# A one-core Perceiver kernel: TensorE multiplies the identity by itself in 24 of its waits

## The reference

```
x = x + _L0_xattn_ref(ctx_1024, _layernorm(x), ...)         # cross attention to 1601 context rows, 16 heads of 64
x = x + _L0_attn_ref(_layernorm(x), ...)                    # selective scan, inner width 256, state 16
x = x + _L0_ffn_ref(_layernorm(x), ...)                     # 4-head attention, then 8 experts, top 2, one shared
x = x + _L1_xattn_ref(ctx_1024, _layernorm(x), mask, ...)   # cross attention, masked
x = x + _L1_attn_ref(_layernorm(x), ...)                    # convolution, state space model, 4 heads, state 64
x = x + _L1_ffn_ref(_layernorm(x), ...)                     # gated feed-forward, inputs and weights rounded to FP4
return x
```

## Time and profile before

| | us |
|---|---|
| median of 3 runs | 2292.67 |
| lowest, highest | 2290.51, 2299.47 |
| profiled execution | 2296.36 |
| its span | 2294.70 |
| TensorE busy in it | 2030.7 (88%) |
| VectorE, ScalarE, GpSimd busy | 1696.9, 1365.7, 566.2 |
| mean granted clock of TensorE | 0.943 of full |

### The profile page before, as it was taken

One profiled execution on the slowest core, in us unless ns is written; L12 is line 12 of the kernel. 1 busy time (PEld: TensorE's weight loads), 2 busy tenths in 40 slices (PEclk: granted clock), 3 DMA queues, 4 the chain that ended last, 5 costly groups with the idle time before them and its releaser, 6 DMA issues. The chain is left out here.

```text
span 2294.7 us, 36359 instructions
## 1 busy us (share of the span) xinstructions
PE 2030.7 (88%) x10794; PEld 1094.3 (48%) x10794; DVE 1696.9 (74%) x4252; ACT 1365.7 (60%) x2461; POOL 566.2 (25%) x584
## 2 busy tenths in 40 slices
PE   5798989998999999979777899999999999997845
PEld 4254535353545354533355354544545454544543
DVE  5778787878787878479656777777786868775456
ACT  3366666666666667644322587778686867776202
POOL 3424343333333331039300201121111111120000
PEclk9799999999999999979888899999999999999877
DMA  2111111111111110023102011111111111100000
GB/s 76 46 46 45 46 46 45 45 45 45 45 45 45 45 45 31 31 70 135 57 1 102 6 35 50 34 53 34 34 34 34 34 34 34 34 31 17 1 10 9
DMA packets 40896, 95.07 MB, mean 41 GB/s; under 512 B 11436, under 2 KB 26776, under 8 KB 40760
## 3 DMA queue, kind: packets, MB, share of 16 engines
q1 hardware_dynamic: 40760, 93.61, 12.0%
HBM read 65.15 MB, written 27.92 MB: 41 GB/s over the span
## 5 line engine op out<-in xcount | busy, mean ns | idle before, releaser
L1063 DVE TENSOR_TENSOR x_p_lo<-x_psum,x_p_hi 128x512 f16<-128x512 f32 (+2 forms) x896 | 605.7, 682 | 207.0 <-ACT x_psum L854 192.4
L853 ACT ACTIVATE x_p_hi<-x_psum 128x512 f16<-128x512 f32 (+2 forms) x480 | 287.9, 600 | 266.2 <-PE x_psum L696 264.4
L716 PE MATMUL x_psum<-x_p_hi,x_x_both 128*128 128x512 f16 (+1 forms) x832 | 318.8, 383 | 58.9 <-DVE x_p_lo L1063 58.7
L853 ACT ACTIVATE x_p_hi<-x_psum,x_bcol 128x512 f16<-128x512 f32 (+1 forms) x416 | 292.3, 703 | 103.9 <-PE x_psum L696 101.6
L694 PE MATMUL x_psum<-x_q,x_xT_both 128*128 128x512 f16 x832 | 320.2, 385 | 6.5 <-DMA x_q<-x_shift_rows 6.5
L695 PE MATMUL x_psum<-x_q,x_xT_both 128*128 128x512 f16 x832 | 318.8, 383 | 0.0
L696 PE MATMUL x_psum<-x_q,x_xT_both 128*128 128x512 f16 x832 | 318.6, 383 | 0.0
L717 PE MATMUL x_psum<-x_p_lo,x_x_both 128*128 128x512 f16 (+1 forms) x832 | 317.8, 382 | 0.0
L718 PE MATMUL x_psum<-x_p_hi,x_x_both 128*128 128x512 f16 (+1 forms) x832 | 317.6, 382 | 0.0
L854 ACT ACTIVATE x_psum<-x_psum 128x512 f32<-128x512 f32 (+2 forms) x480 | 287.3, 598 | 0.6
L1006 DVE CUSTOM_DVE_ANT_0 x_junk<-x_psum,x_brow 128x512 bf16<-128x512 f32 (+2 forms) x512 | 280.1, 586 | 4.7 <-PE x_psum L769 3.8
(11 more groups left out here) (431 smaller groups left out, 3103.3 us busy)
## 6 DMA issues: line engine op xcount, KB each, us to landing
context_rows<-x_x_both SPq DMA_DIRECT2D x16, 832.0 KB, 3.5
context_cols<-x_xT_both SPq DMA_DIRECT2D x16, 832.0 KB, 5.9
x_xT_both<-context_cols SPq DMA_DIRECT2D x16, 832.0 KB, 4.5
x_x_both<-context_rows SPq DMA_DIRECT2D x16, 832.0 KB, 6.3
x_raw<-in_ctx SPq DMA_DIRECT2D x16, 768.0 KB
ssm_c_row<-ssm_bc_rows SPq DMA_DIRECT2D x16, 512.0 KB, 4.2
ssm_b_wide<-ssm_bc_rows SPq DMA_DIRECT2D x7, 512.0 KB, 3.6
x_mrow<-in_mask_BxS_bk SPq DMA_DIRECT2D x16, 200.1 KB
```

The source lines that it names most:

```text
L716: pe.matmul(out, v_hi, p_hi[r][rows, :], start=start, stop=False)
L853: act.activation(p_hi[r][rows, :], score[r][rows, :], ACT.Exp, scale=SCORE_UNIT, **bias).then_inc(p_hi_ready, 1)
L1063: v.tensor_tensor(p_lo[r][rows, :], score[r][rows, :], p_hi[r][rows, :], ALU.subtract).then_inc(p_lo_ready, 1)
```

## The change

A new function issues n float32 products of `ident` with itself, 128 columns each, to one place in a PSUM bank, each overwriting the last. Nobody reads the results, no semaphore is counted, and the next real product into the bank overwrites it. It is called at 20 places of TensorE's code. Two of these are in `cross_attention` with other counts for the masked block, so that 24 calls run, with 371 products. No other engine's code is changed.

```diff
+def keep_clock(pe, bank, ident, n):
+    for _ in range(n):
+        pe.matmul(bank[:, 0:P], ident[:, :], ident[:, :], start=True, stop=True)
...
@@ cross_attention @@
+                    keep_clock(pe, slot_psum[3], ident, 24 if masked else 10)
                     pe.wait_ge(fold_ready, 1)
...
                     pe.wait_ge(lat_ready, 1)
                     pe.wait_ge(prep_dve, 8)
+                    keep_clock(pe, slot_psum[3], ident, 0 if masked else 8)
                     pe.wait_ge(prep_act, 9)
...
                         ins = pe.transpose(slot_psum[1][:, t * P:(t + 1) * P], latx[:, t, :], ident[:, :])
                     ins.then_inc(prep_ready, 1)
+                    keep_clock(pe, slot_psum[3], ident, 8)
...
@@ attention_loop @@
                 if kind == "turn":
+                    if isinstance(at, Pre):
+                        keep_clock(pe, aux[:, 512:1024], ident, 14)
                     pe.wait_ge(m_ready, at.n + 1)
...
                     aux_item(at, item)
+                keep_clock(pe, acc[0], ident, 14)
                 for u in range(AHEAD):
                     scores(u, 0, 0, 0, 0)
...
@@ selective_scan @@
+                keep_clock(pe, slot[1], ident, 12)
                 pe.wait_ge(in_in, 16)
...
                 ins.then_inc(in_turned, 1)
+                keep_clock(pe, slot[1], ident, 6)
                 pe.wait_ge(rest_in, 48)
...
                 ins.then_inc(turned, 1)
+                keep_clock(pe, slot[1], ident, 5)
                 pe.wait_ge(fold_ready, 1)
...
@@ expert_block @@
+                keep_clock(pe, slot[3], ident, 22)
                 pe.wait_ge(heads_in, HEADS_IN)
...
                 ins.then_inc(turned, 1)
+                keep_clock(pe, slot[3], ident, 5)
                 pe.wait_ge(wt_ready, 1)
...
                 product(slot[3], WT[:, K4, :], nxT, k_made)
+                keep_clock(pe, slot[0], ident, 5)
...
+                keep_clock(pe, slot[1], ident, 28)
                 pe.wait_ge(xf_ready, 1)
...
                 ins.then_inc(xf_turned, 1)
+                keep_clock(pe, slot[1], ident, 5)
                 pe.wait_ge(xfT_ready, 1)
...
@@ state_space_block @@
+                keep_clock(pe, slot[3], ident, 24)
                 pe.wait_ge(matrices_in, MATRICES_IN)
...
+                keep_clock(pe, slot[3], ident, 5)
                 pe.wait_ge(wt_ready, 3)
...
+                keep_clock(pe, slot[2], ident, 36)
                 pe.wait_ge(yn_ready, 1)
...
                     ins.then_inc(y_turned, 1)
+                keep_clock(pe, slot[1], ident, 10)
                 pe.wait_ge(yg_ready, 2)
...
@@ fp4_block @@
+                keep_clock(pe, slot[3], ident, 60)
                 pe.wait_ge(u_ready, 1)
...
                 ins.then_inc(u_turned, 1)
+                keep_clock(pe, slot[3], ident, 30)
                 pe.wait_ge(wq_ready, 1)
...
                 ins.then_inc(w_turned, 1)
+                keep_clock(pe, slot[3], ident, 4)
                 pe.wait_ge(w_out, 2)
```

## The result

| | before | changed |
|---|---|---|
| median of 6 runs each, us | 2294.89 | 2278.07 |
| lowest, highest | 2290.51, 2303.24 | 2275.24, 2283.43 |
| profiled execution (span) | 2296.36 (2294.70) | 2277.59 (2275.9) |
| mean granted clock | 0.943 | 0.969 |
| TensorE busy | 2030.7 | 2092.7 |

The changed kernel takes 0.9926 of the time, 95% interval 0.9911 to 0.9941: 17 us less (14 to 20), under one per cent. The sum of the prediction was 14.9 and its forecast 2278. The three runs of the kernel before on which the forecast was built have a median of 2292.67; the six here have 2294.89.

The account below looks back on a forecast made before the run. Most stage-end stretches were taken as engine-to-engine chains with TensorE at half clock. Terms 3.4 + 4.0 + 3.7 + 3.0 + 1.4 + 1.7 - 1.0 - 1.3 = 14.9 us, from median 2292.67 to 2278; range 2269 to 2289.

Parts of the forecast that it names:

- late and early places: Late: expert block's later part, state-space end, last block, 11.1 us gained; early: block starts and maxima's turns, 3.8 us.
- Late part 3.7: Expert block, 28 products ahead of 1166.10: transposes 1.97 to 0.97, product 6.26 to 3.60, 3.7 us gained.
- Start 3.0: Expert block's start, 22 products: 3.9 us gained if the clock holds, nothing if it falls; taken as 3.0.
- End 4.0, start 0: State-space block: end gains 4.0 us (1.3 transposes, 2.7 matmuls); start gains 0, between -2 and +1.5.
- The sum said 3.4: Last block: transposes gain 1.1 us and the first two steps of lines 2156 and 2157 gain 2.3, together 3.4.
- After that the vector engine sets the pace: Last block, after the quantization at 2256.45: the vector engine sets the pace; total gain stays 3.4 us.
- a term of 1.4: Scan's start, 12 products: matmuls of 994.11 shorten from 6.92 to 5.3 us; gain taken as 1.4, between -1.5 and +2.5.
- turn and scores -1.3: Second attention block: products ahead of the maxima's turn cost 1.9 us, first exponential comes 0.6 earlier, net loss 1.3.
- +1.0 said: First attention block: 0.3 - 0.8 + 1.4 - 1.9, the last for the maxima's turn, a loss of 1.0 us.
- 0.3 - 0.8 + 1.4 = 0.9: First attention block's start: first 10 products gain 0.3 us, 8 ahead of 39.04 cost 0.8, the next 8 gain 1.4.
- that same load hides it: First attention block, 14 products behind the turn: scores run at full clock, but the raw-context load hides that gain.
- The falling clock: Rival: clock falls in the 1 to 2 us between products and work; 7 of 15 us stay, 2286; chance 0.19.

Follow-up runs that it names:

- e_early: Changed kernel without the products of the late places, so only those at the five block starts and two turns; 2292.27 us, 0.9976 of the kernel before.
- e_late_shift: Kernel before with the late places' products and, of the early ones, only the 14 behind the turn of the maxima; 2291.04 us, 0.9971 of the kernel before.
- e_late: Kernel before with only the late places' products (28, 5, 36, 10, 60, 30, 4); 2284.94 us, 0.9949 of the kernel before.
- e_plus: Changed kernel with counts removed or trimmed at starts and turns, and products added ahead of attention outputs and the last four tiles; 2277.04 us, 0.9915 of the kernel before.
- e_overrun: Changed kernel with 16 more products in each of three late waits (44, 52, 46 for 28, 36, 30); 2285.79 us, 0.9958 of the kernel before.
- the repeat: Changed kernel run once more, unaltered; 2275.96 us, 0.9919 of the kernel before.
- e_long_only: Changed kernel without the short runs of 4 to 10 products in scan, expert, state-space and last blocks; 2288.05 us, 0.9966 of the kernel before.
- e_transpose: Changed kernel with each added product replaced by two float32 transposes of the identity; 2278.91 us, 0.9917 of the kernel before.

## Why the prediction was right, and where it was not

**The forecast and its mechanism** held: a gain of 14.9 against 17 (14 to 20), and the split into late and early places, 11.1 and 3.8, against 11.7 and 5.5. That 2278 meets 2278.07 to a tenth of a microsecond is luck: the three runs it was counted from lie 2.2 us below the median of the six, and misses of several us in single blocks cancel. The late places' 11.7 is in part luck too, since 2.7 us of its profile's gain lie in a block without products.

**Expert block.** Late part 3.7: the block differs by 3.8 between e_early and the changed kernel. Start 3.0: the scores' matmuls come 14.19 us after entry for 18.67, 4.5 earlier, but 0.9 of it is the weights' landing, 6.03 for 6.93, which is no doing of the products. Some 0.8 is given back until `xf` is turned: TensorE pauses 1.47 us with nothing to wait for, and the 16 transposes behind run at half, 3.51 for 1.97. Against e_late_shift, with the same landing, the start is worth 2.8. (The prediction's good case was added up as 3.9; its terms, 1.7 and 2.4, make 4.1.)

**State-space block.** End 4.0, start 0, measured 3.9 together, 4.4 in e_late with the end alone and 0.8 the other way in e_early with the start alone. The 24 products end 2.5 us past the former landing (2111.89 is 8.08 after entry, 5.52 before), and line 1871 begins 0.4 later, as bounded.

**Last block.** The sum said 3.4, and at the fifth tile it was that (37.83 us after entry for 41.17). The step that failed is "After that the vector engine sets the pace": the end is TensorE's again, and the clock, kept in the profile before over an idle 3.32, fell behind 3.48 in the changed kernel. 1.4 of the 3.4 were lost; e_plus got them back. Since e_early lost the same 1.4 without any product in this block, and e_overrun lost the clock over the very same 3.32, these 1.4 us are not shown to come from the change: it may be the one profile of the kernel before that was lucky.

**Scan.** 12 matmuls 5.51 for 6.92, their end 1.15 us earlier against a term of 1.4. In three of the eight profiles with this block as in the changed kernel (products in fours and transposes in their place included) it takes 136.1 us, in the other five 137.4 to 137.6, more than the 137.0 of the kernel before, e_late and e_late_shift. The mean of the eight is 137.0: of this term nothing is left when the block is over.

**Second attention block.** Start as said: the big product 0.9 later and 1.8 shorter, line 751's first 32 at 3.81 for 5.44. For turn and scores -1.3 was set against this start; the scores came 1.1 us earlier than before where the terms give 0.4. The turn's products cost 1.5 of the 1.9. The block's own 1.9 says little: in e_late, without products, it is shorter still (887.8), and in eight profiles with this block as in the changed kernel it takes 887.1 to 890.5 us.

**First attention block.** The largest miss, +1.0 said and -3.3 measured. Two steps were mis-sized: the start gave 1.4 (the last maximum stands 67.46 us after entry for 68.89) where 0.3 - 0.8 + 1.4 = 0.9 was said, and the turn cost 1.05 (VectorE waited 1.60 for 0.55), the lower bound of 1.1, where 1.9 was taken. One step failed, "that same load hides it": with the products behind the turn the load is used 8.10 us after its issue instead of 9.60, and so 1.9 earlier after entry (80.22 for 82.11); why it comes faster stays open. And 1.6 came from the outputs at full clock by chance, which the repeat doesn't have. Its block of 974.5 is still 2.0 shorter than the one before; the eight profiles with all of this block's products have 971.4 to 975.3, the three kernels without products at its start 975.7 to 976.5.

**The falling clock**, given 0.19 as a rival, is real. It takes longer gaps than those the change leaves in most places, and in e_long_only gaps of 1.3 and 1.5 us were enough. The case against that rival was one row, the idle 3.17; the short runs, which the prediction gave little, keep it away here, since without them 9.2 us of the gain go.

## What to carry to other kernels

Where a TensorE stage is a chain of waits at half clock, unread products in the waits buy back the float32 work behind them, as long as they end inside the wait: past its end each costs its full duration. Price each place by the work behind it at half against full, expect most where the clock is full on entry (at the scan's and the state-space start, entered at half, nothing was left), and don't leave out the small runs in short waits. Compare single profiles block by block and repeat them: chance moves of the clock and of the steady loops here are 1.6 and 6 us, a tenth and a third of the gain.

## What the runs showed of the hardware

- Float32 transposes can raise the granted clock like matmuls: in e_transpose it goes from 0.50 to 1.00 under 24 of them, and 742 in place of 371 products give the same time (0.9917 and 0.9926). In one run of 60, behind an idle 2.09 us, it was 0.53 for the first 3.5 us.
- Behind gaps of 3.92, 3.97 and 4.86 us the clock was at half. Behind 2.82 and 3.17 it was full. Behind 3.15 and 3.48 it was full at first and fell within the next microsecond; over 3.32 it was kept in the kernel before and lost in e_overrun. At one gap of 1.49 us and one of 1.30 it was lost all the same. The length of the gap alone doesn't tell.
- In profiles with products at the expert block's start TensorE stops for 0.65 to 1.75 us within 64 matmuls of 32 columns with nothing to wait for, and for 0.66 with a quarter of the added instructions; in the three kernels without products there it doesn't.
- The landing of the expert block's weights lies at 6.0 to 6.1 us after entry in ten profiles and at 6.9 to 7.8 in four, with and without products at that start.
